# Graph layers over 128 small graphs: the order of ScalarE's last three operations in a step

## The reference, cut to what matters

```
h    = layer input                       # before layers 0 and 2: relu(layernorm(x))
u    = h h^T / sqrt(384);  a = softmax(u);  delta = a * adj
attn = delta / (sum(delta) + 1e-10)
hl, hs, hr = h Wl^T + bl,  h Ws^T + bs,  h Wr^T + br
ctx  = (attn above the diagonal) hl + diag(attn) * hs + (attn below it) hr
o    = relu(layernorm(ctx) * gamma + beta)
```

## Time and profile before

| | |
|---|---|
| median of 3 runs | 1350.23 us (1349.41 to 1350.88) |
| the profiled execution | 1348.79 us |
| its span, first to last instruction | 1346.6 us |
| TensorE matmuls (PE), busy | 1308.3 us, 97% of the span |
| TensorE weight loads (PEld), busy | 1257.5 us, 93% |
| VectorE (DVE), busy | 1093.9 us, 81% |
| ScalarE (ACT), busy | 856.1 us, 64% |
| GpSimd (POOL), busy | 339.1 us, 25% |
| granted TensorE clock, mean | 0.995 of full speed |
| DMA | 44 GB/s over the span |

### The profile page before, as it was taken

How to read it: one execution, slowest core, us unless ns; L and a number is a source line. 1 busy time by engine, 2 the same in 40 slices (tenths; PEclk the granted TensorE clock), 3 DMA queues, 4 the chain that set the end, 5 groups by cost and what they waited for, 6 DMA issues and landing times.

```text
span 1346.6 us, 27781 instructions
## 1 busy us (share of the span) xinstructions
PE 1308.3 (97%) x7820; PEld 1257.5 (93%) x7820; DVE 1093.9 (81%) x3116; ACT 856.1 (64%) x2141; POOL 339.1 (25%) x438
## 2 busy tenths in 40 slices
PE   7999999999999999999999999999999999999997
PEld 6999999999999999999999999999999999999997
DVE  5888888888887777787777778788888888888887
ACT  5666666666666666665666666666666666666664
POOL 1322222222223321111121111232322232232221
PEclk8999999999999999999999999999999999999999
DMA  4111111111011111011110101311011010101101
GB/s 144 59 32 47 31 47 31 47 31 47 31 53 62 47 32 47 31 35 43 31 47 31 47 31 38 100 44 36 32 43 35 31 47 31 47 31 43 35 33 51
DMA packets 44931, 59.26 MB, mean 44 GB/s; under 512 B 3552, under 2 KB 44128, under 8 KB 44896
## 3 DMA queue, kind: packets, MB, share of 16 engines
q1 hardware_dynamic: 44896, 58.83, 13.6%
HBM read 46.24 MB, written 12.58 MB: 44 GB/s over the span
## 4 chain that ended last, share of the span: by engine, by line
PE 84%; issue 6%; DVE 5%; ACT 3%; DMA 1%; ACTq 0%; DVEq 0%; SPq 0%; POOL 0%; POOLq 0%
PE right_bank L396 19%; PE left_bank L396 19%; PE context_bank L396 19%; PE context_bank L439 15%; PE score_bank L368 5%; PE node_bank L356 4%; PE score_bank L376 1%; DVE context L743 1%; PE edge_bank L388 1%; DVE stats L724 1%; ACT context_bank L550 1%; ACT side_parts L538 1%; ACT left_bank L532 1%; DVE side_parts L719 1%; DVE score L655 1%
## 5 line engine op out<-in xcount | busy, mean ns | idle before, releaser
L396 PE MATMUL right_bank<-weight,node_t 128*128 128x384 f32 x1728 | 365.8, 351 | 0.9 <-ACT source L492 0.9
L396 PE MATMUL left_bank<-weight,node_t 128*128 128x384 f32 x1728 | 363.9, 350 | 0.0
L396 PE MATMUL context_bank<-weight,node_t 128*128 128x384 f32 x1728 | 345.8, 341 | 0.0
L396 PEld LDWEIGHTS left_bank<-weight,node_t 128*128 128x128 f32 x1728 | 296.3, 189 | 9.8
L396 PEld LDWEIGHTS context_bank<-weight,node_t 128*128 128x128 f32 x1728 | 300.8, 188 | 3.2
L396 PEld LDWEIGHTS right_bank<-weight,node_t 128*128 128x128 f32 x1728 | 291.1, 189 | 11.4 <-issue 1.0
L439 PE MATMUL context_bank<-side_parts,attn_t 128*128 128x384 f32 x1152 | 247.4, 349 | 25.0 <-issue 16.3
L439 PEld LDWEIGHTS context_bank<-side_parts,attn_t 128*128 128x128 f32 x1152 | 192.6, 188 | 46.5 <-issue 29.8
L538 ACT ACTIVATE side_parts<-right_bank 128x384 fp32r<-128x384 f32 x192 | 93.0, 484 | 140.8 <-PE context_bank L439 140.8
L864 POOL TENSOR_TENSOR rstd<-spread,scalars 128x2 f32<-128x2 f32 x96 | 90.1, 939 | 352.3 <-DVE spread L735 352.3
L550 ACT ACTIVATE context_bank<-context_bank,diag 128x384 f32<-128x384 f32 x192 | 104.2, 543 | 98.1 <-PE context_bank L396 98.1
(11 more groups left out here) (62 smaller groups left out, 1668.0 us busy)
## 6 DMA issues: line engine op xcount, KB each, us to landing
rows<-x SPq DMA_DIRECT2D x32, 384.0 KB, 3.3
adj_in<-adj SPq DMA_DIRECT2D x96, 128.0 KB, 2.1
residual_x<-x SPq DMA_DIRECT2D x32, 384.0 KB, 3.1
out<-rows SPq DMA_DIRECT2D x31, 384.0 KB, 2.5
piece<-weights SPq DMA_DIRECT2D x18, 192.0 KB, 2.7
rows<-weights SPq DMA_DIRECT2D x3, 576.0 KB, 8.6
vector_rows<-vectors SPq DMA_DIRECT2D x3, 576.0 KB, 5.6
vector_rows<-vectors SPq DMA_DIRECT2D x3, 384.0 KB, 6.0
```

The lines of the kernel that those rows point to most:

```text
L396: mm = nc.tensor.matmul(bank[:, 0:D], node_t[:, s.parity, k, c, a], weight[:, s.phase % 2, w, c, b], start=False, stop=(c, a) == (CH - 1, ...
```

## The change

It reorders three calls at the end of ScalarE's `body(s)`. `scale_self(s, 1)` moves from the last place to the place behind `seed_self(nxt, 0)`, then comes `seed_side(nxt, 0, LEFT)`, and `fill_source(after, 1)` is last. No instruction is added, removed or resized, and no other engine's list is touched.

```diff
                 if nxt.exists():
                     seed_self(nxt, 0)
+                scale_self(s, 1)
+                if nxt.exists():
+                    seed_side(nxt, 0, LEFT)
                 if after.exists():
                     fill_source(after, 1)
-                if nxt.exists():
-                    seed_side(nxt, 0, LEFT)
-                scale_self(s, 1)
```

## The result

| | median | ratio to before (95% interval) |
|---|---|---|
| before | 1349.82 us, 4 runs (1349.41 to 1350.88) | |
| changed | 1307.09 us, 4 runs (1306.45 to 1307.75) | 0.9682 (0.9666 to 0.9699) |

The change takes 42.7 us off, 3.2%. The forecast was 1322.3 us and a range from 1310 to 1336: right side, right mechanism, and too little by a third.

What follows compares the result with a forecast made beforehand. TensorE was taken as the bound, stalled before the weighing by ScalarE's late scaling. Phase gains 11.5 + 5.2 + 11.2 = 27.9 us took the profiled 1348.79 to 1320.9, with 1.44 added for the median 1322.3 us; range 1310 to 1336.

Steps and rivals of the forecast that it cites:

- The reading of the bottleneck: TensorE idles before the weighing (L439), 46.5 us on the weight-load row, because the scaling (L550) is last in ScalarE's list.
- issue: Rival: L439 stalls labelled so are TensorE's own instruction handling and stay; 13.9 us gain at most, 1336.3 us, chance 0.05.
- The scaling in time, the two others covered: ScalarE's new order: stall goes whole with 0.32 us to spare; left bias rows cost nothing; source fill has 0.63 us cover.
- price of a stall: Each stall before L439 costs its weight-load idle less 0.07 us; phase 0 gives 11.5 us, phase 1 gives 5.2.
- VectorE's play: Phase 2: VectorE limits the gain to 11.2 us, 8.3 from its weighing wait and 2.9 from its turned-scores wait.
- ceiling of 22.1 us: Upper bound of the phase 2 term: 24.4 us of idle in 33 stalls, less 0.07 us each.
- full recovery of 38.8 us: Stall costs before L439 over all three phases together, if every one were recovered; gives 1311.4 us.
- The stretch at the border of the phases: Stall-free step between phases 0 and 1, 13.16 us, taken to agree with phase 2's 13.84 - 0.70 = 13.14.
- All stalls go: Rival: VectorE keeps pace in phase 2, all 38.8 us recovered, 1311.4 us; chance 0.13.
- VectorE gives less: Rival: nothing gained in phase 2 and half of phase 0; gain 11.0 us, 1339.2 us; chance 0.14.
- nothing moves: Rival: the weighing's true release is another condition at the same moment, such as VectorE's side part; 1350 us, chance 0.03.
- The slower rival: Left projection waits for the moved source fill; breaks even at 0.29 us wait a step, 1361 us at 0.4; chance 0.03.

Runs made afterwards that it cites:

- half moves: Kernel before, with the scaling moved ahead of the left bias rows only (1317.43 us), or ahead of the source fill only (1312.88 us).
- eight points: Weight-load idle per step against step excess over a stall-free step, from the kernel before and three edits: both half moves and the doubled left bias copy.

## Why the prediction was wrong

Going by its own steps:

- **The reading of the bottleneck was right.** The stalls before `weigh(s, 1)` were the scaling's, also those put down to "issue": 46.5 us became 1.6, half moves gave back parts of about the size of the move, and doubling a copy in front of the scaling added its duration in every phase.
- **The scaling in time, the two others covered: right,** though the 0.32 us of spare time were a number of the kernel before: with VectorE lagging, the slower steps of phase 2 have none of it. The stall went whole, and moving the scaling further changed nothing. The source fill had cover, and one more place later it had none (0.26 us a step).
- **Two terms of the sum failed in size.** By phase, 14.8, 7.9 and 19.6 us came where the sum has 11.5, 5.2 and 11.2. Of the 14.4 us by which it was short, 6.0 lie in phases 0 and 1, which rest on the price of a stall alone, and 8.4 in phase 2, which rests on VectorE's play alone.
- **The price of a stall, "its idle time less 0.07 us for each stall".** The runs show its idle time plus 0.04, over eight points. The 0.26 us between two first matmuls was right (216.96 to 217.22), but I had taken it as all there is to a free passage and missed what comes after: from the weighing to the left projection a stalled step took 1.14 us, a free one takes 1.04. And a free weight load starts 0.08 us before the one ahead of it ends, so that the zero of the idle row is not the free state. Over the 59 stalls of phases 0 and 1 the 0.11 us make 6.5 us, which is what they were short by. In phase 2 the price doesn't enter the sum, but it set the ceiling of 22.1 us (25.7 at the measured price) and, through the full recovery of 38.8 us, the low end of the range. The stretch at the border of the phases, 13.16 us, was read as agreement with 13.14; the free step is 13.08.
- **The size of VectorE's play in phase 2, "VectorE allows 8.3 + 2.9 = 11.2 us".** That VectorE is next was right: cutting its work brought 13.27 down to 13.09. But it held back 0.18 us a step, some 6 us, not 10.9, and 19.6 us came through. Going through its waits: the one for the weighing went as foretold, by 7.7 us (8.3 to 0.6). The one for the turned scores fell by 8.1 us (11.2 to 3.1), but 6.8 came back as `in_shift`'s wait for GpSimd, so the pair gave 1.3 where I had allowed 2.9. The wait for ScalarE's node part, which I had said stays, fell by 3.5 us (4.9 to 1.4). And some play was in no listed wait at all. Below are VectorE's instructions around the weighing, and the ScalarE instruction (L538) that the second needs, before and then after:

```profile
1108.34 0.56 DVE L724 BATCH_NORM_STATS2 stats<-context_bank 128x6 f32<-128x384 f32 x1 [0.40 <-PE context_bank L439]
1108.40 0.49 ACT L538 ACTIVATE side_parts<-right_bank 128x384 fp32r<-128x384 f32 x1 [1.20 <-PE context_bank L439]
1108.92 0.56 DVE L719 TENSOR_TENSOR side_parts<-right_bank,side_parts 128x384 fp32r<-128x384 f32 x1
```

```profile
1075.32 0.49 ACT L538 ACTIVATE side_parts<-right_bank 128x384 fp32r<-128x384 f32 x1 [0.18 <-PE context_bank L439]
1075.79 0.55 DVE L724 BATCH_NORM_STATS2 stats<-context_bank 128x6 f32<-128x384 f32 x1
1076.26 0.54 DVE L719 TENSOR_TENSOR side_parts<-right_bank,side_parts 128x384 fp32r<-128x384 f32 x1
```

  From start to start 0.58 us before and 0.47 after, with no idle time listed for the second in either, and so it is in nearly every step of phase 2: 0.11 us a step, 3.5 over the phase. Before, L719 did wait: ScalarE's side part ended at 1108.89, 0.03 us ahead of it, because it had itself waited for the late weighing. After, it ended at 1075.81, long in time: L719 starts at 1076.26, 0.08 us before L724 ends (1075.79 + 0.55). Neighbours on VectorE overlap like this when nothing is waited for, and a wait that does little more than eat the overlap is not listed. These four parts, 7.7 + 1.3 + 3.5 + 3.5, make an estimate of 16 of the 19.6 us; where the rest sits wasn't followed up.
- **The rivals.** "All stalls go", with 0.13, was nearest; its 1311.4 us was 4 us too high, as it has the wrong price of a stall. It is not true in full, as phase 2 keeps 0.19 us a step, nearly all of it VectorE's. "VectorE gives less" and the two on "issue" and "nothing moves" fell. The slower rival was a real mechanism, in the right place; its break-even was never near.
- **The range** took in the unknown play of VectorE and left the price of a stall as if it were known. Had the full recovery been priced by the weight-load row as it stands, 45.2 us in the earlier trace rows, the low end would have been 1350 - 45 = 1305, and the time inside.

On the rule cited in the prediction (the Trainium skill, "Perfetto Trace Analysis", Identifying the Most-Contended Engine): the weight-load row is the better measure of headroom, and the eight points agree, with idle and excess within 0.09 us of each other. The matmul row's 25.0 us was much too low against the 42.3 that came.

## What to carry to other kernels

In an engine's hand-written order, put ahead what another engine waits for next, and last what has the longest cover; check the moved operation's cover one place further, as the next one may be the cliff. When one stall is repeated in every step, price it by the difference of step lengths with and without it, not by the gap between two instructions: the recovery behind a stall costs too. And before a second engine is priced as the limit, compare its starts with and without waits: what it can make up is more than its listed waits say.

## What was not expected of the hardware

A stall of TensorE costs more than shows as idle on its weight-load row: 0.03 to 0.09 us more at six of the eight points (0.01 and 0.02 less at the other two). In the free passage the weight load runs 0.17 us ahead of its matmul (217.05 and 217.22), in the stalled one 0.03 (1106.97 and 1107.00). The Trainium skill ("TensorE: Matmul & The Clock Gate", Step-by-step: what each phase is for) says that TensorE pulls weight loads ahead of matmuls in flight. The rows agree: the load at 217.05 starts inside the matmul of 216.96. A weighing held by a semaphore gives up that lead and, it seems, earns it back only over its six matmuls; that last point is read off the 1.14 against 1.04 us and wasn't tested by itself.

The "issue" label is no verdict. Of the 46.5 us of stalls 29.8 were put down to it (the page's row; the earlier trace rows have 28.6 of them), and all but 1.2 went with the move of one instruction of ScalarE. What the label does mark is a longer hand-over. In the looped steps of the kernel before, two of which are written out per round, the two labels come in turn. From the end of the scaling to the weight load it is 0.17 to 0.18 us in all 54 stalls put down to "issue" (1106.79 to 1106.97 in the earlier trace rows) and 0.05 us in all 39 put down to L550; the next step after that of the earlier trace rows is one of these:

```profile
1120.23 0.53 ACT L550 ACTIVATE context_bank<-context_bank,diag 128x384 f32<-128x384 f32 x1
...
1120.81 0.30 PEld L439 LDWEIGHTS context_bank<-side_parts,attn_t 128*128 128x128 f32 x2 [0.72 <-ACT context_bank L550]
```

So in 54 of the 93 stalls some 0.13 us more lay between the end of the scaling and the weight load, 7 us in all. It went with the stalls, but what it is made of isn't shown by any run here.
